# Feed forwards of eight experts: down products in three rounded parts, with the up products three units ahead

## The reference, cut to what matters

```
h = silu(einsum('td,edf->tef', x, w1)) * einsum('td,edf->tef', x, w3)
out_e = einsum('tef,efd->ted', h, w2)
out = einsum('ted,te->td', out_e, combine)
```

## Time and profile before

| | us |
|---|---|
| three runs | 4869.35, 4881.72, 4894.25 |
| median | 4881.72 |
| profiled execution | 4872.02 |
| its span, first to last instruction | 4868.9 |
| PE busy in the span | 4144.8 |
| DVE busy | 2692.0 |
| ACT busy | 1977.6 |
| POOL busy | 1699.3 |

### The profile page before, as it was taken

How to read it: one execution, slowest core, us unless ns; L and a number is a source line. 1 busy time by engine, 2 the same in 40 slices (tenths; PEclk the granted TensorE clock), 3 DMA queues, 4 the chain that set the end, 5 groups by cost and what they waited for, 6 DMA issues and landing times. The chain is left out here.

```text
span 4868.9 us, 88104 instructions
## 1 busy us (share of the span) xinstructions
PE 4144.8 (85%) x27774; PEld 2925.8 (60%) x27774; DVE 2692.0 (55%) x4164; ACT 1977.6 (41%) x3118; POOL 1699.3 (35%) x1336
## 2 busy tenths in 40 slices
PE   8899999999997988867877999999695666666799
PEld 4578888888885765743444555555353444453477
DVE  4344454544543443544655565663538999978343
ACT  2255555555551223212432555554233444430222
POOL 2256656666552323200432224320033333320042
PEclk8899999999997989879887999999697888788699
DMA  2000000000000110511002222231001101100011
GB/s 89 1 10 10 20 20 10 20 10 20 20 1 28 60 41 1 128 32 50 2 1 59 59 65 64 60 68 32 1 1 41 28 23 28 28 16 0 6 60 49
DMA packets 124779, 153.98 MB, mean 32 GB/s; under 512 B 86928, under 2 KB 110240, under 8 KB 124224
## 3 DMA queue, kind: packets, MB, share of 16 engines
q1 hardware_dynamic: 124352, 148.54, 12.0%
HBM read 110.25 MB, written 2.66 MB: 23 GB/s over the span
## 5 line engine op out<-in xcount | busy, mean ns | idle before, releaser
L1052 POOL TENSOR_TENSOR pexp_lo<-arena,pexp_hi 128x800 fp32r<-128x800 f32 x384 | 635.3, 1655 | 437.3 <-POOLq L1051 437.3
L2278 DVE TENSOR_REDUCE arena<-ps 128x1 f32<-128x482 f32 (+3 forms) x624 | 393.1, 657 | 361.7 <-DVEq L2256 350.7
L2400 DVE TENSOR_REDUCE arena<-ps 128x1 f32<-128x482 f32 (+3 forms) x624 | 399.8, 657 | 267.5 <-DVEq L2386 259.5
L1546 ACT ACTIVATE arena<-ps 128x800 f32<-128x800 f32 x384 | 322.1, 839 | 494.8 <-ACTq L1544 492.8
L1646 ACT ACTIVATE arena<-ps 128x800 f32<-128x800 f32 x384 | 316.2, 837 | 256.5 <-ACTq L1645 254.4
L998 POOL TENSOR_TENSOR max_diag<-w_const,arena 100x800 fp32r<-100x800 f32 x160 | 246.7, 1542 | 443.7 <-POOLq L996 443.7
L2593 DVE MATCH_REPLACE8 arena<-arena 128x1444 f32<-128x1444 f32 x208 | 341.3, 1650 | 0.0
L3318 PE MATMUL ps<-k_hi,q_by_head 128*128 128x482 f32 (+3 forms) x624 | 291.5, 471 | 45.6 <-PEq L3274 42.2
L1547 ACT ACTIVATE pexp_hi<-ps 128x800 fp32r<-128x800 f32 x384 | 319.6, 832 | 0.0
L2695 DVE TENSOR_TENSOR arena<-ps,arena 128x400 f32<-128x400 f32 x256 | 147.1, 575 | 279.0 <-DVEq L2694 279.0
L2051 DVE TENSOR_REDUCE arena<-ps 100x8 f32<-100x800 f32 x160 | 158.3, 991 | 258.4 <-DVEq L2048 258.4
(11 more groups left out here) (398 smaller groups left out, 9259.2 us busy)
## 6 DMA issues: line engine op xcount, KB each, us to landing
ctxT<-in_ctxT SPq DMA_DIRECT2D x56, 541.5 KB
kst<-k_hi SPq DMA_DIRECT2D x128, 180.5 KB, 3.1
ctxk<-in_ctx SPq DMA_DIRECT2D x40, 528.0 KB
chunk<-in_ff_chunks SPq DMA_DIRECT2D x77, 193.0 KB, 2.4
arena<-gate_dram SPq DMA_DIRECT2D x64, 200.0 KB, 3.9
kst<-xn SPq DMA_DIRECT2D x64, 180.5 KB, 2.9
arena<-gate_dram SPq DMA_DIRECT2D x64, 100.0 KB, 2.6
arena<-in_ctxT SPq DMA_DIRECT2D x8, 541.5 KB
```

What stands on the lines that cost most here:

```text
L1052: own(nc.gpsimd.tensor_tensor(pexp_lo[p % 3][:, :, :], pexp[p % 3], pexp_hi[p % 3][:, :, :], ALU.subtract))
L1546: nc.scalar.activation(pexp[p % 3], of, ACT.Exp, scale=scale).then_inc(s.pexp_ready, 1)
L2278: peak = nc.vector.tensor_reduce(mparts[0:at.stop - at.start, m, c:c + 1], bank(k, z - a, at.stop - at.start), AX.X, ALU.max)
L2400: peak = nc.vector.tensor_reduce(mparts2[0:n, m, c:c + 1], bank(k, z - a, n), AX.X, ALU.max)
```

## The change

The down product of the eight-expert stages becomes three rounded matmuls. The split of the weight chunks takes all 384 columns. ACT writes the high half of `h_all` (`hidden_high`), DVE the low half (`hidden_low`), each one unit behind silu and product; four buffers of each lie in free columns of the cross attention's weight buffer. The up products run three units ahead of the down products, and wait for `h_ready`; the down products wait for `low_there`. DVE waits for its own product before it signals ACT and PE. Some semaphores are renamed, and `picks` shares one with the cross weights.

```
-    w_hi, w_lo = [[rounded_in_arena(f"w_{k}{c}", [128, 256]) for c in range(4)] for k in ("hi", "lo")]
+    w_hi, w_lo = [[rounded_in_arena(f"w_{k}{c}", [128, 384]) for c in range(4)] for k in ("hi", "lo")]
+    h_at = w_cross_at + 4 * 4000
+    h_hi, h_lo = [[rounded(f"h_{k}{i}", [128, GT], h_at + 4 * GT * (4 * part + i)) for i in range(4)] for part, k in enumerate(("hi", "lo"))]
...
-            sp.dma_start(picks, dram["picks"]).then_inc(s.picks_loaded, 16)
+            sp.dma_start(picks, dram["picks"]).then_inc(loaded["picks"], 16)
...
-                split(w_hi[c][:, :], w_lo[c][:, :], chunk[c][:, 0:256])
+                split(w_hi[c][:, :], w_lo[c][:, :], chunk[c][:, 0:384])
...
+            def hidden_high(u):
+                act.wait_ge(s.h_there, 1)
+                act.sem_inc(s.h_there, -1)
+                nc.scalar.activation(h_hi[u % 4][:, :], h_all[u % 2], ACT.Copy).then_inc(s.high_ready, 1)
+
             if cfg["gate"] == "block":
-                for i in range(cfg["loop"]):
-                    block(range(4))
...
+                for u in range(4 * NG * cfg["E"]):
+                    act.wait_ge(s.up_done, 1)
+                    act.sem_inc(s.up_done, -1)
+                    nc.scalar.activation(h_act[u % 2], bank(u % 2), cfg["func"]).then_inc(s.h_act_ready, 1)
+                    if u > 0:
+                        hidden_high(u - 1)
+                hidden_high(4 * NG * cfg["E"] - 1)
...
+            def hidden_low(u):
+                dve.wait_ge(s.high_ready, 1)
+                dve.sem_inc(s.high_ready, -1)
+                nc.vector.tensor_tensor(h_lo[u % 4][:, :], h_all[u % 2], h_hi[u % 4][:, :], ALU.subtract).then_inc(s.dve_done, 1)
+                dve.wait_ge(s.dve_done, 1)
+                dve.sem_inc(s.dve_done, -1)
+                dve.sem_inc(s.low_there, 1)
...
-                    nc.vector.tensor_tensor(h_all[u % 2], bank(2 + u % 2), h_act[u % 2], ALU.mult).then_inc(s.h_ready, 1)
-                    if u // NG == 2 and i + 1 < cfg["E"]:
+                    nc.vector.tensor_tensor(h_all[u % 2], bank(2 + u % 2), h_act[u % 2], ALU.mult).then_inc(s.dve_done, 1)
+                    dve.wait_ge(s.dve_done, 1)
+                    dve.sem_inc(s.dve_done, -1)
+                    dve.sem_inc(s.h_there, 1)
+                    dve.sem_inc(s.h_ready, 1)
+                    if u > 0:
+                        hidden_low(u - 1)
+                    if u // NG % 4 == 2 and i + 1 < cfg["E"]:
                         scaled(i + 1, u % NG)
...
+            def down_parts(c, g, u, last):
+                pe.wait_ge(s.low_there, 1)
+                pe.sem_inc(s.low_there, -1)
+                to, hi, lo = bank(4 + g), w_hi[c][:, 256:384], w_lo[c][:, 256:384]
+                mm(to, hi, h_hi[u % 4][:, :], start=False, stop=False)
+                mm(to, hi, h_lo[u % 4][:, :], start=False, stop=False)
+                downed(mm(to, lo, h_hi[u % 4][:, :], start=False, stop=last), c, g, last)
...
+                def up_next(u):
+                    pe.wait_ge(s.h_ready, 1)
+                    pe.sem_inc(s.h_ready, -1)
+                    c, g, i = units[u]
+                    up(c, g, u % 2, i)
+
+                up_next(2)
+                for u, (c, g, i) in enumerate(units):
+                    if u + 3 < len(units):
+                        up_next(u + 3)
+                    down_parts(c, g, u, i + 1 == cfg["E"] and c == 3)
```

More of the change, by code:

```diff
@@ L106, in __init__ @@
         self.ctx_bf_free = made("ctx_bf_free")
-        self.pexp_hi_ready = made("pexp_hi_ready")
-        self.pexp_hi_there = made("pexp_hi_there")
-        self.pexp_lo_ready = made("pexp_lo_ready")
+        self.high_ready = made("high_ready")
+        self.high_there = made("high_there")
+        self.low_there = made("low_there")
         self.fold_w = made("fold_w")
@@ L165, in __init__ @@
         self.slot_free = made("slot_free")
-        self.picks_loaded = made("picks_loaded")
+        self.h_there = made("h_there")
 SELF = {
@@ L428, in build @@
     loaded["masks"] = loaded["const"]
-    loaded.update(dict.fromkeys(CROSS, ctx.enter_context(nc.semaphore("loaded_cross"))))
+    loaded.update(dict.fromkeys([*CROSS, "picks"], ctx.enter_context(nc.semaphore("loaded_cross"))))
     ctx_loaded = [ctx.enter_context(nc.semaphore(f"ctx_loaded_{i}")) for i in range(2)]
@@ L617, in build @@
     x_hi, x_lo = [rounded_in_arena("x_" + k, [128, T]) for k in ("hi", "lo")]
-    w_hi, w_lo = [[rounded_in_arena(f"w_{k}{c}", [128, 256]) for c in range(4)] for k in ("hi", "lo")]
+    w_hi, w_lo = [[rounded_in_arena(f"w_{k}{c}", [128, 384]) for c in range(4)] for k in ("hi", "lo")]
+    h_at = w_cross_at + 4 * 4000
+    assert max(dram[k].shape[1] for k in ("ca1", "ca2")) <= 4000 and 4000 + 8 * GT <= w_cross.shape[1]
+    h_hi, h_lo = [[rounded(f"h_{k}{i}", [128, GT], h_at + 4 * GT * (4 * part + i)) for i in range(4)] for part, k in enumerate(("hi", "lo"))]
     xg_hi, xg_lo = [[rounded(f"xg_{k}{i}", [128, T], arena_at + 4 * (pairs_at + T * (2 * part + i))) for i in range(2)]
@@ L1049, in lows @@
                 pool.sem_inc(s.pexp_ready, -1)
-                pool.wait_ge(s.pexp_hi_ready, 1)
-                pool.sem_inc(s.pexp_hi_ready, -1)
+                pool.wait_ge(s.high_ready, 1)
+                pool.sem_inc(s.high_ready, -1)
                 own(nc.gpsimd.tensor_tensor(pexp_lo[p % 3][:, :, :], pexp[p % 3], pexp_hi[p % 3][:, :, :], ALU.subtract))
-                pool.sem_inc(s.pexp_lo_ready, 1)
+                pool.sem_inc(s.low_there, 1)
                 pool.sem_inc(s.pexp_free, 1)
@@ L1547, in exponents @@
                 own(nc.scalar.activation(pexp_hi[p % 3][:, :, :], of, ACT.Exp, scale=scale))
-                act.sem_inc(s.pexp_hi_ready, 1)
-                act.sem_inc(s.pexp_hi_there, 1)
+                act.sem_inc(s.high_ready, 1)
+                act.sem_inc(s.high_there, 1)
             def batch(par, first=False, more=True):
@@ L1763, in film_block @@
             queries(1)
-            act.wait_ge(s.picks_loaded, 16)
-            act.sem_inc(s.picks_loaded, -16)
+            act.wait_ge(loaded["picks"], 16)
+            act.sem_inc(loaded["picks"], -16)
             for n in range(TILES // 2):
@@ L1819, in block @@
                         s.h_act_ready if cfg["up2"] else s.h_ready, 1)
+            def hidden_high(u):
+                act.wait_ge(s.h_there, 1)
+                act.sem_inc(s.h_there, -1)
+                nc.scalar.activation(h_hi[u % 4][:, :], h_all[u % 2], ACT.Copy).then_inc(s.high_ready, 1)
             if cfg["gate"] == "block":
-                for i in range(cfg["loop"]):
-                    block(range(4))
-            elif cfg["loop"]:
+                for u in range(4 * NG * cfg["E"]):
[5 more added lines that the diff above has]
+                hidden_high(4 * NG * cfg["E"] - 1)
+                return
+            if cfg["loop"]:
                 with act.Fori(0, cfg["loop"]) as i:
@@ L2689, in scaled @@
                 dve.sem_inc(gate_free[g], 1)
+            def hidden_low(u):
[5 more added lines that the diff above has]
+                dve.sem_inc(s.low_there, 1)
             def expert(i):
-                for u in range(4 * NG):
+                for u in range(4 * NG * i, 4 * NG * i + 4 * NG):
                     dve.wait_ge(s.h_act_ready, 1)
                     dve.sem_inc(s.h_act_ready, -1)
-                    nc.vector.tensor_tensor(h_all[u % 2], bank(2 + u % 2), h_act[u % 2], ALU.mult).then_inc(s.h_ready, 1)
-                    if u // NG == 2 and i + 1 < cfg["E"]:
+                    nc.vector.tensor_tensor(h_all[u % 2], bank(2 + u % 2), h_act[u % 2], ALU.mult).then_inc(s.dve_done, 1)
[6 more added lines that the diff above has]
+                    if u // NG % 4 == 2 and i + 1 < cfg["E"]:
                         scaled(i + 1, u % NG)
@@ L2725, in feed_forward @@
                     expert(i)
+                hidden_low(4 * NG * cfg["E"] - 1)
             elif cfg["up2"]:
@@ L3197, in values @@
                     pe.sem_inc(s.u_free, -1)
-                pe.wait_ge(s.pexp_hi_there, 1)
-                pe.sem_inc(s.pexp_hi_there, -1)
+                pe.wait_ge(s.high_there, 1)
+                pe.sem_inc(s.high_there, -1)
                 for i in range(2):
@@ L3208, in values_lo @@
                 g = p // PAIRS
-                pe.wait_ge(s.pexp_lo_ready, 1)
-                pe.sem_inc(s.pexp_lo_ready, -1)
+                pe.wait_ge(s.low_there, 1)
+                pe.sem_inc(s.low_there, -1)
                 for i in range(2):
@@ L3589, in down, with downed @@
                 ins = mm(bank(4 + g), chunk[c][:, 256:384], h_all[k], start=False, stop=last)
+                downed(ins, c, g, last)
+            def down_parts(c, g, u, last):
+                pe.wait_ge(s.low_there, 1)
+                pe.sem_inc(s.low_there, -1)
+                to, hi, lo = bank(4 + g), w_hi[c][:, 256:384], w_lo[c][:, 256:384]
```

(11 more changed lines are left out.)

## The result

The changed kernel takes 5006.55 us (median; 5000.27 to 5019.68) beside 4885.1 us of the kernel before (4869.35 to 4894.25): a ratio of 1.0262 over the runs, with a 95% interval of 1.024 to 1.0284 (the two medians alone make 1.0249). Each kernel ran four times. The forecast was 5022 us in a range of 4974 to 5070. The profiled execution took 5000.27 us; its span is 4998.1 us.

What follows compares the result with a forecast made beforehand. PE bounded both stages before and DVE would after: plain units, 28 us of scalings and 24 of POOL's blocking make 297.1 us, less 229.5, plus 2.35 = +70 a stage, +140 in all: 5022 us, range 4974 to 5070.

Steps and rivals of the forecast that it cites:

- plain units: Eight-expert stages: DVE needs 0.575 + 0.44 + 0.566 + 0.35 = 1.93 us a unit, over PE's 1.62, 127 intervals a stage.
- scalings: DVE's token scalings for the next expert, hidden by PE before, add 1.01 us each, 28 us a stage.
- POOL's blocking: POOL's splits hold back DVE's SBUF subtractions: 24 us a stage, bounds 0 and 47 us.
- Chains: DVE's semaphore instructions: four behind the product leave it idle 0.44 us, three behind the subtraction 0.35 us.
- rival 1: Faster: semaphore instructions are absorbed in DVE's operations and PE stays the bound in both stages; 4851 us, chance 5%.
- rival 2: No change: a chain on DVE costs only its first 0.15 us; 4882 us, chance 3%.
- weight splits: POOL's four weight splits an expert meet DVE's subtraction at random points: 0.3 us each, 1.2 us an expert.
- Subtraction: DVE's new subtraction, estimated from the token scaling and another tensor's split: 0.566 us.
- ACT, waits and tables: ACT's copy and the new waits cost nothing while DVE is the bound; ACT about 1.4 us a unit.
- Rival 3: ACT reloads its tables between silu and copy, a unit of 4.0 us; 5440 us, chance 3%.
- Rival 4: PE's gaps let its clock fall to 1.2 GHz for good, a unit of 2.97 us; 5180 us, chance 5%.
- Tail: After a stage's last product, two subtractions precede the closing additions: 2.35 us later than before.

Runs made afterwards that it cites:

- light chain: The change, but product and subtraction signal their own completion, ACT and PE wait for one count, h_all has four buffers: 4914.76 us, ratio 1.006 to before.
- the run with 8 columns: The change with ACT's copy of the high half cut to 8 of 400 columns from the fifth unit on: 5019.26 us, one execution.

## Why the prediction was right

The bound moved to DVE, as forecast, and each term can be read off. A stage from first to last product:

| term | forecast, us | measured in the first stage, us |
|---|---|---|
| plain units | 127 x 1.93 = 245.1 | 127 x 1.94 = 246.4 |
| scalings | 28 | 28 x (0.575 + 0.44) = 28.4 |
| POOL's blocking | 24 | 128 x (0.713 - 0.577) = 17.4 |
| gaps, not foreseen (last section) | 0 | 9 x 0.35 = 3.2 |
| sum | 297.1 | 295.4, of 296.1 |

That the sum comes within 1 us of the stage is in part luck: POOL's term was 6.6 us too large, and 4.9 us that were missing elsewhere made up for most of it.

**Chains.** The 0.44 and 0.35 of the earlier trace rows stand unchanged in their new places, and two instructions more cost 0.19. That settles rival 1 (absorbed) and rival 2 (only the first costs). The Trainium skill, "VectorE: DVE Perf Modes", section "The DRAIN you can't avoid", has a semaphore after each operation at no extra cost. The light chain agrees for a completion that the operation signals itself: 0.49 us from product to subtraction, with a wait for ACT between them. So a semaphore instruction is not dear by itself. The change pays because DVE waits for its own completion: that wait leaves it 0.15 us idle, and each semaphore instruction behind it adds 0.095. For such chains the trace does not agree with the section.

**POOL.** The mechanism was right, the size 7 us a stage too large. Added up over the 128 subtractions of the first stage, the time above 0.577 us is 12.4 us beside POOL's splits of scaled tokens (forecast 7 x 2.0 = 14) and 5.1 beside its splits of weights (forecast 8 x 1.2 = 9.6). So the mis-sized term is above all the meeting with the weight splits, 0.64 us an expert in place of 1.2: I had let it fall at random, and it falls on the same few of an expert's 16 units. Held subtractions mostly took 1.02 us; the forecast's 1.3 was seldom reached (1.18 at the most in the first stage, 1.33 in the second). The run with POOL idle gives back 15 of the 17.4, the rest being its first experts. As forecast, the product, which reads PSUM, is never stretched (576 ns at most). The scaling, 1.30 at worst in the earlier trace rows, now mostly starts when POOL is quiet and takes 0.88 at most in the first stage; the delay went to the subtraction. The wider split takes POOL 0.50 and 1.01 us, for the estimated 0.51 and 1.0:

```profile
L1285 POOL CAST w_hi<-chunk x27: 502/505/878, 1579.6 to 1819.7; 128x384 fp32r<-128x384 f32 x27
L1285 POOL TENSOR_TENSOR w_lo<-chunk,w_hi x27: 1000/1014/1313, 1580.3 to 1820.4; 128x384 fp32r<-128x384 f32 x27
```

**Subtraction.** 0.577 in place of 0.566 us, 1.4 us a stage; 0.566 was that of a scaling that starts while the product is in flight, 0.574 that of a split behind a semaphore instruction. The subtraction shows the same two values: median 0.577 behind the change's chain, 0.565 in the light chain.

**ACT, waits and tables.** ACT's copy costs nothing, as the run with 8 columns shows, and DVE does not wait for it: the 0.44 us before the subtraction are those of the chain. Rival 3 falls: ACT loads a table once, ahead of the stage, and silu and copy alternate at 0.50 and 0.53 us, where a reload would take 1.28.

**Clock.** Rival 4 did not come: the stages were granted 0.98 and 0.99. Once in the first stage, right behind a burst of scalings (from 1655.73 us), PE's matmuls were 0.33 us apart for some 3 us. The prediction had such a fall covered in the units with a scaling; it came in the plain ones behind them, and DVE's pace hid all but 0.26 us of it (the product at 1660.59 waited 0.61 us, for silu, in place of 0.35). That a lasting fall is possible here shows in the run two units ahead, with PE busy 401.73 of 752.90 us at a granted clock of 0.58.

**Tail.** From the last product to the last addition, start to start, 5.37 us in place of 2.98 (1776.04 to 1779.02): 2.4 more, for the forecast 2.35.

```profile
1843.91 0.57 DVE L2717 TENSOR_TENSOR arena<-ps,arena 128x400 f32<-128x400 f32 x1 [0.35 <-DVEq L2716]
...
1849.28 0.57 DVE L2769 TENSOR_TENSOR x<-ps,x 128x400 f32<-128x400 f32 x1 [0.26 <-DVEq L2761]
```

**The sum.** Stages and tails give 66.6 + 65.8 + 2 x 2.4 = 137 us, for the forecast 140. The profiled executions differ by 128.2 (5000.27 - 4872.02), the medians by 121.5. The missing 9 us lie in code that the change leaves alone but for renamed semaphores: from the last product of the first stage to the first of the second it was 2855.4 us before (1776.0 to 4631.4) and 2848.5 after (1843.9 to 4692.4), although 2.4 of that are the tail's. In the experiments this stretch took up to 2871 us, and the first product came between 1546.5 and 1561.6 us, in the same code. What moves it was not tried and stays open (runs of the kernel before alone lie 25 us apart); it is why I judge the runs by their stages first. Of the light chain's 27 us over the kernel before, 13 are in its stages.

**A miss in an expectation.** For the light chain I took PE's unit as cover for the scalings, by the sum of DVE's own work. That left out that DVE and POOL take turns, so that four scalings in a row make a loop with a length of its own.

## What to carry to other kernels

Work that is moved to an engine with idle time has the price of its whole unit there: each wait for the engine's own completion counts, with every wait or signal that stands behind it as an instruction of its own (here seven in all, 0.79 of 1.94 us), and so does every neighbour with which it takes turns. Let operations signal their own completion. A burst that one bound has hidden comes out when that bound gets shorter, so spread it before counting on the gain.

## What the runs showed of the hardware that was not expected

After each 128 instructions of DVE, counted in the trace with its semaphore instructions, the gap from a semaphore instruction to the next instruction is 0.42 to 0.44 us instead of 0.07 to 0.09. In the first stage with POOL idle nine such gaps lie 128 instructions apart, or 256 at the one place where none shows. On DVE's timeline it is the 0.70 here, where the same chain else takes 0.35:

```profile
1711.47 0.57 DVE L2719 TENSOR_TENSOR arena<-ps,arena 128x400 f32<-128x400 f32 x1 [0.35 <-DVEq L2718]
1712.48 0.57 DVE L2710 TENSOR_TENSOR h_lo<-arena,h_hi 128x400 fp32r<-128x400 f32 x1 [0.44 <-DVEq L2709]
1713.76 0.57 DVE L2719 TENSOR_TENSOR arena<-ps,arena 128x400 f32<-128x400 f32 x1 [0.70 <-DVEq L2718]
```

Where DVE is the bound this costs 9 x 0.35 = 3.2 us a stage. What causes it was not tried.

The turns between DVE and POOL go both ways: POOL's subtraction of scaled tokens, 1.04 us in the change, took 1.39 in the light chain, where DVE's subtraction was first. The 1.382 at most of the earlier trace rows had shown the same before the change.
